# Two input buffers instead of resident x, and the blanks of the slots filled in the weights' tiles, in a top-2 mixture-of-experts stage

## The reference

```python
xf = layernorm(x)                                   # 8 x 512 x 256 tokens, T = 4096
scores = softmax(xf @ w_router)                     # 8 experts
expert_weights, expert_indices = top_k(scores, 2)
h = silu(xf @ w1[e]) * (xf @ w3[e]); y = h @ w2[e]  # hidden 512, per chosen expert e
shared = silu(xf @ ws1) * (xf @ ws3) @ ws2
out = shared / 3 + (sum of expert_weight * y) * 2 / 3
x = x + layernorm(out)
```

## Time and profile before

| | |
|---|---|
| three runs | 5072.12, 5128.7 and 5144.03 us, median 5128.7 |
| the profiled execution | 5128.7 us, its span 5127.0 us, mean granted clock 0.887 |
| TensorE busy over the span | 4101.3 us (80%) |
| VectorE, ScalarE, GpSimd busy | 2496.6, 1998.0, 2022.4 us |
| last stage | from about 4415 us to the end of the span |
| TensorE busy in it | 625.66 of 712 us |

### The profile page before, as it was taken

One profiled execution on the slowest core, in us unless ns is written; L12 is line 12 of the kernel. 1 busy time (PEld: TensorE's weight loads), 2 busy tenths in 40 slices (PEclk: granted clock), 3 DMA queues, 4 the chain that ended last, 5 costly groups with the idle time before them and its releaser, 6 DMA issues. The chain is left out here.

```text
span 5127.0 us, 65161 instructions
## 1 busy us (share of the span) xinstructions
PE 4101.3 (80%) x23438; PEld 2832.8 (55%) x23438; DVE 2496.6 (49%) x4367; ACT 1998.0 (39%) x3621; POOL 2022.4 (39%) x2049
## 2 busy tenths in 40 slices
PE   5698779658999970993688876967988888799995
PEld 2576367435666650992344444535666667655663
DVE  5432561224444448224456552227889888511222
ACT  3212412232332320222455551227888888212222
POOL 4424032221222220664112211117999889441223
PEclk9767887779999985996899998988999999799998
DMA  4631161110000024995344321010121111632224
GB/s 124 201 118 31 34 208 38 55 69 10 9 17 9 9 68 146 264 297 148 102 119 124 91 77 60 29 47 28 44 64 52 48 46 48 193 107 68 46 46 122
DMA packets 311729, 438.12 MB, mean 85 GB/s; under 512 B 68870, under 2 KB 225862, under 8 KB 307286
## 3 DMA queue, kind: packets, MB, share of 16 engines
q1 hardware_dynamic: 288902, 403.60, 25.7%
q0 software_dynamic: 22512, 30.36, 3.2%
HBM read 303.84 MB, written 130.03 MB: 85 GB/s over the span
## 5 line engine op out<-in xcount | busy, mean ns | idle before, releaser
L3136 POOL TENSOR_TENSOR mamba_hC<-mamba_h_t,mamba_cb 128x512 f32<-128x512 f32 x512 | 671.4, 1338 | 81.9 <-DVE mamba_h_t L2689 80.0
L2689 DVE TENSOR_TENSOR_SCAN mamba_h_t<-mamba_dA,mamba_pB 128x512 f32<-128x512 f32 x512 | 596.5, 1206 | 118.8 <-PE mamba_pB L3028 54.9
L3028 PE MATMUL mamba_pB<-ident,mamba_dBT 128*128 128x128 f32 x2048 | 326.4, 283 | 57.8 <-DVE mamba_h_t L2689 51.9
L2845 ACT ACTIVATE mamba_dA<-mamba_delta,mamba_a_neg 128x512 f32<-128x512 f32 x512 | 358.1, 716 | 13.1 <-DVE mamba_h_t L2689 12.3
L3028 PEld LDWEIGHTS mamba_pB<-ident,mamba_dBT 128*128 128x128 f32 x2048 | 239.2, 144 | 193.6 <-issue 106.4
L3037 PE MATMUL mamba_pY<-ident,mamba_hC 128*128 128x128 f32 x2048 | 319.7, 280 | 17.7 <-POOL mamba_hC L3136 15.6
L1667 POOL TENSOR_SCALAR mqa_prob<-mqa_prob,mqa_rinv 128x128 f32<-128x128 f32 (+3 forms) x256 | 137.6, 538 | 484.4 <-DVE mqa_rinv L1464 483.8
L2034 DVE TENSOR_REDUCE mha_nmax<-mha_pM 128x1 f32<-128x384 f32 (+3 forms) x352 | 217.2, 639 | 223.8 <-PE mha_pM L2316 221.2
L1525 ACT ACTIVATE mqa_prob<-mqa_pS,mqa_nmax 128x128 f32<-128x128 f32 (+3 forms) x256 | 134.9, 527 | 458.7 <-DVE mqa_nmax L1458 458.7
L2153 ACT ACTIVATE mha_prob<-mha_pW 128x512 f32<-128x512 f32 (+1 forms) x352 | 191.0, 562 | 231.4 <-PE mha_pW L2334 229.6
L1458 DVE TENSOR_REDUCE mqa_nmax<-mqa_pS 128x1 f32<-128x128 f32 (+3 forms) x256 | 124.8, 488 | 315.5 <-PE mqa_pS L1605 312.8
(11 more groups left out here) (564 smaller groups left out, 9448.4 us busy)
## 6 DMA issues: line engine op xcount, KB each, us to landing
expert_w<-in_L_ffn_W SPq DMA_DIRECT2D x48, 1024.0 KB
delta_shared<-delta_w SPq DMA_DIRECT2D x64, 576.0 KB, 4.6
mamba_cb<-mamba_c SPq DMA_DIRECT2D x128, 256.0 KB, 3.1
mha_qkT<-mha_parts_d SPq DMA_DIRECT2D x96, 256.0 KB
delta_w<-delta_wst SPq DMA_DIRECT2D x32, 576.0 KB, 2.8
expert_w<-in_L_ffn_W SPq DMA_DIRECT2D x48, 256.0 KB
top_w<-in_L_ffn_w SPq DMA_DIRECT2D x24, 512.0 KB
top_slots<-top_y SPq DMA_DIRECT2D x1, 9159.0 KB, 43.1
```

The costliest lines, as they stand in the source:

```text
L2689: nc.vector.tensor_tensor_scan(h_t[:, n % RH, :], dA[:, n % RA, :], pB[n % 2][:, :], 0.0, ALU.mult, ALU.add).then_inc(z["scan_ready"], 1)
L2845: nc.scalar.activation(dA[:, n % RA, :], delta[:, a % 2, ct, :], ACT.Exp, scale=a_neg[:, ct, s:s + 1])\
L3028: last = nc.tensor.transpose(pB[n % 2][:, tok(t)], dBT[:, r % RS, t, ct * P:(ct + 1) * P], c.ident[:, :])
L3136: nc.gpsimd.tensor_tensor(hC[:, n % RO, :], h_t[:, n % RH, :], cb[:, r % RC, :], ALU.mult)\
```

## The change

x is loaded into the two halves of `x_in` instead of eight places in `w2`; the third and later loads each wait until `scale` of the batch two before is done. The shared weights are issued right after the first batch. The blank rows are now made in the heads of `w1`, `w3` and `w2`, 24 rows in each partition of each: VectorE fills each with a memset behind `scale` of batches 0, 1 and 2, POOL writes the ids with three iotas after rstd of batch 3, and SP writes them to `slots_d` with three DMAs of 24, 24 and 23 tiles, behind the last load of x. SP waits until these have landed before it issues the expert weights, which overwrite them. The wait of these weights for the end of the norm part goes, and so does the pacing of the scatters.

```diff
--- before.py
+++ after.py
@@ -823,6 +823,7 @@
     DVE_ROWS = tuple(b for b in range(NB) if b not in POOL_ROWS)
     RING = 4
     XRING = 8
+    BLANK = (TILES + 2) // 3
     slots_d = nc.dram_tensor("top2_slots", [TILES * P, W_ROW], F32, kind="Internal").ap()
     sum_d = nc.dram_tensor("top2_sum", [T + P, D], F32, kind="Internal").ap()
     with Scope(nc, "top2") as sc:
@@ -869,7 +870,7 @@
                 "t_g_ready", "t_h_ready", "hT_ps", "hT_ready", "t_y_ps", "t_y_ready", 
                 "base_st", "y_var", "y_scale", "yn_ready", "x_out_p", "x_out_v", "dch", "consts", "blank")
         z = {s: sc.sem(s) for s in sems}
-        x_ready = [sc.sem(f"x_ready{b}") for b in range(NB)]
+        x_ready = [sc.sem(f"x_ready{i}") for i in range(2)]
         y_in = [sc.sem(f"y_in{b}") for b in range(NB)]
         xr_in, x_stored = sc.sem("xr_in"), sc.sem("x_stored")
         xg_in = [sc.sem(f"xg_in{i}") for i in range(XRING)]
@@ -877,8 +878,8 @@
         wr_in, ws_in = sc.sem("wr_in"), sc.sem("ws_in")
         rows_of = lambda a: a.rearrange("(b p t) d -> b p t d", t=NT, p=P)
         rows_in = lambda a: a.rearrange("b (p t) d -> b p t d", t=NT)
-        blank = y[:, :, :].rearrange("p i d -> p (i d)")[:, 0:W_ROW]
-        x = w2[:, 0:E * JH, :].rearrange("p (b t) d -> p b t d", t=NT)
+        blanks = [(i * BLANK, min((i + 1) * BLANK, TILES), t.rearrange("p a d -> p (a d)")[:, 0:BLANK * W_ROW]
+                   .rearrange("p (i d) -> p i d", d=W_ROW)) for i, t in enumerate((w1, w3, w2))]
         total = w3.rearrange("p a d -> p (a d)")[:, 0:NB * NT * D].rearrange("p (b t d) -> p b t d", b=NB, t=NT)
         xres = w1.rearrange("p a d -> p (a d)")[:, 0:NB * NT * D].rearrange("p (b t d) -> p b t d", b=NB, t=NT)
         pR = bank[4][:, 0:TT * E].rearrange("p (t e) -> p t e", e=E)
@@ -901,17 +902,20 @@
             def _(sp):
                 sp.dma_start(wr[:, :, :], w["L3_ffn_w_router"].rearrange("(k p) e -> p k e", p=P)).then_inc(wr_in, 16)
                 for b in range(NB):
-                    sp.dma_start(x[:, b, :, :], rows_in(src)[b]).then_inc(x_ready[b], 16)
-                for t, one, k in ((w1, "L3_ffn_ws1", KD), (w3, "L3_ffn_ws3", KD), (w2, "L3_ffn_ws2", JH)):
-                    sp.dma_start(t[:, E * k:, :], w[one].rearrange("(k p) h -> p k h", p=P)).then_inc(ws_in, 16)
-                sp.wait_ge(z["blank"], 2)
-                sp.dma_start(slots_d.rearrange("(i p) d -> p i d", p=P), blank.unsqueeze(1).to_broadcast([P, TILES, W_ROW]))\
-                    .then_inc(z["spare_in"], 16)
-                sp.dma_start(sum_d[T:T + P, :], blank[:, 0:D]).then_inc(z["spare_in"], 16)
+                    if b >= 2:
+                        sp.wait_ge(z["xn_ready"], b - 1)
+                    sp.dma_start(x_in[:, b % 2, :, :], rows_in(src)[b]).then_inc(x_ready[b % 2], 16)
+                    for t, one, k in ((w1, "L3_ffn_ws1", KD), (w3, "L3_ffn_ws3", KD), (w2, "L3_ffn_ws2", JH)):
+                        if b == 0:
+                            sp.dma_start(t[:, E * k:, :], w[one].rearrange("(k p) h -> p k h", p=P)).then_inc(ws_in, 16)
+                sp.wait_ge(z["blank"], 6)
+                for first, end, t in blanks:
+                    sp.dma_start(slots_d[first * P:end * P, :].rearrange("(i p) d -> p i d", p=P), t[:, 0:end - first, :])\
+                        .then_inc(z["spare_in"], 16)
+                sp.dma_start(sum_d[T:T + P, :], blanks[0][2][:, 0, 0:D]).then_inc(z["spare_in"], 16)
+                sp.wait_ge(z["spare_in"], 16 * 4)
                 for e in range(E):
                     for t, many_w, k in ((w1, "L3_ffn_w1", KD), (w3, "L3_ffn_w3", KD), (w2, "L3_ffn_w2", JH)):
-                        if e == 0 and t is w2:
-                            sp.wait_ge(z["xn_ready"], NB)
                         sp.dma_start(t[:, e * k:(e + 1) * k, :],
                                      w[many_w][e].rearrange("(k p) h -> p k h", p=P)).then_inc(z["w_in"], 16)
                 sp.wait_ge(z["sent"], 16 * TOP * TT)
@@ -947,9 +951,9 @@
                 link = Chain(dve, z["dch"]).link
 
                 def stats(b):
-                    dve.wait_ge(x_ready[b], 16)
-                    for t in range(NT):
-                        last = nc.vector.bn_stats(stat[:, b % 2, t, :], x[:, b, t, :])
+                    dve.wait_ge(x_ready[b % 2], 16 * (b // 2 + 1))
+                    for t in range(NT):
+                        last = nc.vector.bn_stats(stat[:, b % 2, t, :], x_in[:, b % 2, t, :])
                     link(last)
                     for t in range(NT):
                         last = nc.vector.bn_aggr(mv[:, b % 2, t, :], stat[:, b % 2, t, :])
@@ -958,7 +962,7 @@
                 def scale(b):
                     dve.wait_ge(z["rstd_ready"], 2 * (b + 1))
                     for t in range(NT):
-                        last = nc.vector.tensor_scalar(xall[:, b * NT + t, 0:D], x[:, b, t, :], mv[:, b % 2, t, 0:1],
+                        last = nc.vector.tensor_scalar(xall[:, b * NT + t, 0:D], x_in[:, b % 2, t, :], mv[:, b % 2, t, 0:1],
                                                        rstd[:, b % 2, t:t + 1], ALU.subtract, ALU.mult)
                     last.then_inc(z["xn_ready"], 1)
 
@@ -967,6 +971,8 @@
                         stats(b)
                     if b >= 1:
                         scale(b - 1)
+                    if 1 <= b <= 3:
+                        nc.vector.memset(blanks[b - 1][2], 0.0).then_inc(z["blank"], 1)
 
                 def shared_product(u):
                     dve.wait_ge(z["g_ready"], u + 1)
@@ -1271,9 +1277,6 @@
                 nc.gpsimd.tensor_scalar(iota_t[:, :], iota_t[:, :], 1.0, 0.0, ALU.mult, ALU.add).then_inc(z["consts"], 1)
                 nc.gpsimd.tensor_copy(xall[:, :, D:D + 1].rearrange("p t a -> p (t a)").bitcast(U32), token[:, :])\
                     .then_inc(z["consts"], 1)
-                nc.gpsimd.memset(blank, 0.0).then_inc(z["blank"], 1)
-                pool.wait_ge(z["blank"], 1)
-                nc.gpsimd.iota(blank[:, D:D + 1].bitcast(U32), [[0, 1]], base=T, channel_multiplier=1).then_inc(z["blank"], 1)
                 for b in range(NB):
                     pool.wait_ge(z["var_ready"], b + 1)
                     nc.gpsimd.tensor_scalar(rstd[:, b % 2, :], mv[:, b % 2, :, 1], EPS, None, ALU.add)\
@@ -1281,7 +1284,13 @@
                     pool.wait_ge(z["rstd_ready"], 2 * b + 1)
                     nc.gpsimd.tensor_tensor(rstd[:, b % 2, :], rstd[:, b % 2, :], c.minus_half[:, 0:NT], ALU.pow)\
                         .then_inc(z["rstd_ready"], 1)
-                pool.wait_ge(z["spare_in"], 16 * 2)
+                    if b == 3:
+                        pool.wait_ge(z["blank"], 3)
+                        for first, end, t in blanks:
+                            ids = t[:, 0:end - first, D:D + 1].rearrange("p i a -> p (i a)").bitcast(U32)
+                            nc.gpsimd.iota(ids, [[0, end - first]], base=T, channel_multiplier=1)\
+                                .then_inc(z["blank"], 1)
+                pool.wait_ge(z["spare_in"], 16 * 4)
                 pool.wait_ge(z["xn_ready"], NB)
                 for i in range(TOP):
                     pool.wait_ge(z["slot_ready"], i + 1)
@@ -1291,8 +1300,6 @@
                                             TOP / (TOP + 1.0), 1.0, ALU.mult, ALU.mult).then_inc(z["id_ready"], 1)
                     pool.wait_ge(z["id_ready"], i + 1)
                     for t in range(TT):
-                        if (i * TT + t) % 3 == 0:
-                            pool.wait_ge(z["h_ready"], 5 + (i * TT + t) // 3)
                         pool.indirect_dma_start(out=slots_d, in_=xall[:, t, :], in_offset=None,
                                                 out_offset=bass.IndirectOffsetOnAxis(ap=slot[i][:, t:t + 1], axis=0))\
                             .then_inc(z["sent"], 16)
```

## The result

| | before | after |
|---|---|---|
| median (lowest to highest), us | 5118.7 (5072.1 to 5144.0) | 5199.3 (5175.1 to 5212.8) |
| ratio, 95% interval | | 1.0149 (1.0109 to 1.0191) |
| profiled execution: time, span | 5128.7, 5127.0 | 5222.5, 5220.8 |
| its granted clock | 0.887 | 0.881 |

A forecast was written before the change was run, and what follows sets the result against it. TensorE was taken to bound all three parts of the last stage. Scatter pacing cost 0, and slower x loading with memsets shifted the norm part 20.5 us: 5128.7 + 20.5 = 5149.2 us (+0.4%), range 5088 to 5173 us.

The forecast's parts named there:

- Cost 0, gain 0: Shared part: unpaced scatters, 1.26 us apart, neither slow TensorE nor help anyone by ending earlier; 0 us.
- The rival of the scatters: Scatters at 3.8 us each would overrun the shared part and end 87 us late, giving 5236 us; chance 0.03.
- within 2% of before: Whole kernel: outcome class holding the forecast, the rival of a rising clock and that of free memsets; chance 0.96.
- The norm part: Start of the last stage: TensorE's last transposes move from 4460.73 to 4481.2, a shift of 20.5 us.
- x(1): Second batch of x, now queued behind three shared weights: its stats start about 5.6 us after those of the first.
- A step with a memset: Norm part, three batches on VectorE: 3.00 us of work plus a 5.22 us memset, 8.22 us each.
- The bare steps: Norm part, three batches without memset: 3.57 us waiting for the load plus 3.09 us of work, 6.66 us each.
- a floor of 10.3: Norm part rival: memsets cost nothing and x(1) is early, yet paced loads shift 10.3 us, 5139.0 us; chance 0.02.
- The clock: Norm part: granted clock stays at 0.50; the rival of a rise gave a shift of 13.0, 5141.7 us; chance 0.04.
- the late blanks and the wait ahead of the weights: Blanks land by 4513.5, expert weights by 4550, needed at 4676 in the tile loop: hidden, cover 126 us.
- the low shift: Norm part, lower bound: x(1) not late and loads of 3.3 us, shift 15.8 us, taken as 16.
- the high one: Norm part, upper bound: x(1) issued fifth and landing late, loads of 4.94 us, shift 28.2 us, taken as 29.

The follow-up runs named there:

- e1: Kernel before, with only the pacing of the scatters (POOL's wait for h_ready before every third) removed; 5158.4 us, ratio 1.0079.
- e8: Changed kernel with pacing back, memsets and iotas moved behind the last scale and rstd, and shared weights issued behind x(1); 5151.4 us.
- e7: Changed kernel with pacing back, the three memsets moved behind the last scale and the iotas behind the last rstd; 5139.5 us.
- e2: Changed kernel with the pacing of the scatters put back and nothing else; 5140.7 us, ratio 1.0057.
- e6: Changed kernel, scatters unpaced but with a 1024-column POOL memset and a wait for it before every third, tied to no unit; 5166.7 us.
- e4: Changed kernel, scatters unpaced but POOL waits for all expert weights to land before the first scatter; 5182.5 us.
- e9: Changed kernel plus a tiny ScalarE copy between its two waits and a tiny VectorE memset waiting for TensorE's signal; 5128.0 us.
- e11: Changed kernel, unpaced, with a 1024-column POOL memset and a wait for it before every twelfth scatter only; 5099.5 us.
- e14: Changed kernel plus only a tiny VectorE memset waiting for TensorE's signal, ScalarE keeping its pair of waits; 5197.4 us.

## Why the prediction was wrong

**The pacing ("Cost 0, gain 0") is the step that failed.** In the profiles it measured 53 us done alone (e1) and 64 with the rest, by the timed runs 40 and 47. The argument was that four units with scatters took as long as four without. That is true, and of scatters 1.87 us apart on average only; the row says nothing of 1.30, the distance that the change makes. The distance inside a group of three, 1.26 us, was taken as proof that POOL can keep that pace. It can, and did: 4530.3 to 4612.3. But its pace was never what was at stake. What the runs showed in place of the zero is a hole in the shared part, in which TensorE waits up to 62.88 us because its own signals reach ScalarE late while the scatters go out 1.27 us apart.

**The rival of the scatters had the sign and the wrong mechanism.** It asked whether they could overrun the shared part, each at up to 3.8 us, and came to +87 us at a chance of 0.03. No scatter became slower, none was late for the tile loop, and it was POOL's neighbours who waited. So +80.6 us near its +107 is no confirmation. Nor is it credit to the working that the time fell within 2% of before, to which it gave 0.96: it did so by a mechanism that is in none of its cases. What was missing is a case in which a faster engine delays others by something that isn't a transfer or a queue of its own; the one weighed for it was contention of DMAs, and that is 0.28 in the hole.

**The norm part held, with one term short.** Forecast +20.5, measured +24.7 us; the difference of 4.2 comes out of three terms. x(1) came 6.42 us behind x(0) (forecast 5.6): +0.8. A step with a memset took 9.41 us (8.22): +3.6 in three. The working took a memset's own record as its cost. The record is as worked out from the earlier trace rows, 5.22 us for 6192 elements, but 1.24 us of idle time ("issue") stand ahead of each, behind `scale` as behind another memset (e8), and they are part of its price: 6.46 us. The earlier trace rows had this already: the memset of 4096 elements has 0.8 us of "issue" ahead of its 3.472, together 1.04 ns for each element, as 6.46 us are for 6192. The bare steps took 6.19 + 6.35 + 7.30 = 19.84 us, forecast 3 x 6.66 = 19.98. The waits for x were 3.17, 3.25 and 4.21 us before `stats` of batches 5, 6 and 7 and none before 2, 3 and 4, where I expected 3.5 to 4 and none. e7 and e8 confirm the pieces: without the memsets 9.6 us less (three steps of 9.41 become bare ones of 6.4, which is 9.0), x(1) early another 4.7, and a rest of 10.4 us where the working had a floor of 10.3.

The Trainium skill (VectorE: DVE Perf Modes, "Zero memsets can be issued as uint32 (trn2)") gives one cycle for each element, from which, with the 0.96 GHz of that page, the prediction's estimate was 6.45 us. This case's trace agrees: 6.46 us from one memset to the next (e8). The prediction set that estimate aside because the rows showed less, which was a misreading of them. With it the forecast shift would have been 3.7 us higher, 24.2, against 24.7 measured.

**The clock** stayed at 0.50 through the norm part, with TensorE busy 41.31 of 71.10 us, as forecast. That it would fall again later was not foreseen: in the hole it is at 0.50, after TensorE stopped, and the first projection behind it takes 3.53 us for eight products instead of 1.99.

**The rest held.** The weights were first issued at 4515.34 and TensorE never waited for them; the tile loop took 407.2 us (408.9 before), and the rest 60.4 (61.5), so the late blanks and the wait ahead of the weights are hidden, as costed.

**The range** reached from the lowest run with the low shift to the highest run with the high one, and with them it treated the price of the pacing as known. From rows in which scatters never stood closer than three together, nothing bounds that price from above; the range should have said so.

**What stays open.** It is shown that taking out the pacing makes the hole and putting it back removes it (e1, e2). It is shown too that TensorE's signals reach ScalarE and VectorE 5 to 61 us late while GpSimd issues indirect DMAs 1.3 us apart, that the signals of ScalarE and VectorE in the same stretch come at once, that time between the scatters cures it (e6) and that weights in flight aren't needed for it (e4). Not shown is what holds the signals, whether on TensorE's side or on their way, why those of TensorE, and why one chip did without (e9). Scatters of another size, or another DMA in their place, were not tried. That the chip is the reason, and not the moment, was not tried: no kernel ran on it twice.

In no version was the last stage shorter than the 708.2 us of the kernel before; e11's one execution of 5099.5 us owes its time to an early start of the stage (4364.5), which took 733.2. The part that a mend could give back is the pacing's (e2); two buffers with no lookahead still cost 10.4 us (e8).

## What to carry to other kernels

A wait that seems to hold up only its own engine may be what keeps others running: before taking one away, look for a stretch in the trace where the engine already runs at the pace that it will then have for as long as it will then last, and where there is none, leave the price open upwards. Two input buffers, loaded only when free, cost the load's whole latency in every batch (3.2 to 3.4 us of 6.4 here), unless something of that length stands beside it. The price of an instruction is the distance from its start to the next one's, not its record alone: idle time that always stands ahead of it and waits for nothing is part of it. And one kernel without an effect is a result only beside the plain kernel on the same chip.

## What the runs showed of the hardware

- While GpSimd issued scatters 1.30 us apart on average, TensorE's semaphore signals came in the changed kernel 4.9, 26.4 and 61.2 us late, from about 13 scatters into the row to 8 us after its end; at 1.62 us apart (e6) or three per unit (e2) none was late. In e9, on one chip, they came in time at 1.30 us.
- Two engines that waited for the same late signal went on within 0.03 us of each other (e14).
- A VectorE memset of 6192 f32 columns has a record of 5.22 us with 1.24 us of idle time ahead of it, each time (nine times in after, e7 and e8), behind a `tensor_scalar` or behind another memset; three in a row started 6.46 us apart (e8).
- In the same stretch other signals were not late: VectorE's product started 0.03 us behind the end of SiLU, at 4552.89 and again at 4579.54, and TensorE's projection 0.05 us behind the end of that product (after).
- A load of 512 KB that is issued only when its buffer is free let its reader start 3.2 to 3.4 us later in e7 and e8.
